# A second set of buffers, a new order of work and smaller on-chip tables in a six-layer local-attention decoder on one Trainium2 core

## The reference

```
x = layernorm(x)
for i in range(6):
    x = attn_layer(shift_tokens(x), Wqkv[i], ...) + x
    x = ffn_layer(shift_tokens(x), ...) + x

attn_layer: q, k, v = split(x @ Wqkv)      # 16 heads of 64
            q, k = l2norm(q) * qs, l2norm(k) * ksc, then rotary tables cos/sin * scale
            out  = softmax(8 q.k within a window of 32 + the 32 before) @ v
            return out @ Wo
ffn_layer:  a, gate = split(layernorm(x) @ W1 + b1)     # 341 each
            return (a * gelu(gate)) @ W2 + b2
result = x_before + that x
```

## Time and profile before

| | |
|---|---|
| median of three runs | 1828.08 us |
| profiled execution, its time | 1832.19 us |
| its span (first to last instruction) | 1830.4 us |
| PE busy | 1636.3 us, 89% |
| DVE busy | 1537.4 us, 84% |
| POOL busy | 1361.2 us, 74% |
| ACT busy | 1188.8 us, 65% |
| stack() begins | at 230.1 us |
| first and last add_attention of a tile | 286.8 and 1784.5 us |

### The profile page before, as it was taken

One profiled execution on the slowest core, in us unless ns is written; L12 is line 12 of the kernel. 1 busy time (PEld: TensorE's weight loads), 2 busy tenths in 40 slices (PEclk: granted clock), 3 DMA queues, 4 the chain that ended last, 5 costly groups with the idle time before them and its releaser, 6 DMA issues.

```text
span 1830.4 us, 77270 instructions
## 1 busy us (share of the span) xinstructions
PE 1636.3 (89%) x32727; PEld 1367.4 (75%) x32727; DVE 1537.4 (84%) x3220; ACT 1188.8 (65%) x2281; POOL 1361.2 (74%) x971
## 2 busy tenths in 40 slices
PE   6688769999989999989999989999899999899985
PEld 4455557788777888878887878888788888788873
DVE  6588779988878999879998979999799899799951
ACT  4465546676666777657767756777676677577651
POOL 4355567788767888778887878888688888788852
PEclk9789979999999999999999999999999999999996
DMA  3644211111221212111213112112112131121101
GB/s 102 253 162 162 81 48 34 41 43 39 92 55 34 54 46 82 53 51 43 54 40 101 40 46 56 47 58 86 43 40 54 40 112 41 45 56 47 37 18 52
DMA packets 81081, 118.47 MB, mean 65 GB/s; under 512 B 41643, under 2 KB 55140, under 8 KB 80612
## 3 DMA queue, kind: packets, MB, share of 16 engines
q1 hardware_dynamic: 80162, 113.27, 21.0%
q10 hardware_dynamic: 578, 0.26, 0.1%
HBM read 38.72 MB, written 21.32 MB: 33 GB/s over the span
## 4 chain that ended last, share of the span: by engine, by line
PE 74%; issue 5%; DVE 4%; DMA 1%; ACT 1%; POOL 1%; SPq 0%; ACTq 0%; DVEq 0%; POOLq 0%
PE banks L1168 10%; PE banks L1181 10%; PE banks L1086 8%; PE banks L1130 7%; PE banks L1088 7%; PE banks L1087 7%; PE banks L1143 5%; PE banks L1098 4%; PE banks L1108 4%; PE banks L1223 4%; PE banks L1198 2%; PE banks L1200 2%; PE banks L1199 2%; DMA wo<-in_L_ffn_Wo_dram 1%; PE banks L1069 1%
## 5 line engine op out<-in xcount | busy, mean ns | idle before, releaser
L1416 POOL TENSOR_TENSOR qk_c<-qk_c,qk_s 128x1024 f32<-128x1024 f32 x192 | 459.2, 2392 | 210.9 <-DVE qk_s L1511 208.1
L1424 POOL TENSOR_TENSOR qk_c<-qk_c,nrm 128x1024 f32<-128x1024 f32 x192 | 362.6, 1905 | 41.0 <-DVE nrm L1559 41.0
L1086 PE MATMUL banks<-high,xT 128*128 128x512 f32 x576 | 270.9, 470 | 19.4 <-DVE qk_s L1511 12.1
L1500 DVE TENSOR_TENSOR qk_c<-banks,rot 128x512 f32<-128x512 f32 x384 | 261.6, 681 | 31.1 <-ACT sq L1289 30.0
L1329 ACT COPY pT<-banks 128x512 f32<-128x512 f32 x192 | 112.7, 587 | 266.2 <-PE banks L1143 266.2
L1511 DVE TENSOR_TENSOR qk_s<-banks,rot 128x512 f32<-128x512 f32 x384 | 261.2, 680 | 0.0
L1289 ACT ACTIVATE sq<-banks 128x512 f32<-128x512 f32 x384 | 237.0, 617 | 23.3 <-PE banks L1088 13.3
L1088 PE MATMUL banks<-high,xT 128*128 128x512 f32 x576 | 231.6, 402 | 0.9 <-issue 0.9
L1518 DVE TENSOR_REDUCE ssq<-sq 128x16 f32<-128x1024 f32 x192 | 232.0, 1208 | 0.0
L1087 PE MATMUL banks<-low,xT 128*128 128x512 f32 x576 | 230.2, 400 | 0.9 <-issue 0.9
L1181 PEld LDWEIGHTS banks<-wo,attT 128*128 128x128 f32 x1536 | 194.9, 200 | 36.5 <-issue 26.3
(11 more groups left out here) (157 smaller groups left out, 3673.7 us busy)
## 6 DMA issues: line engine op xcount, KB each, us to landing
v_back<-v_own SPq DMA_DIRECT2D x96, 384.0 KB, 3.7
front_raw<-in_L_ffn_Wqkv_dram SPq DMA_DIRECT2D x18, 512.0 KB, 5.5
v_back<-v_own SPq DMA_DIRECT2D x72, 128.0 KB, 2.4
w_high<-high SPq DMA_DIRECT2D x15, 512.0 KB, 2.7
w_low<-low SPq DMA_DIRECT2D x15, 512.0 KB, 4.1
high<-w_high SPq DMA_DIRECT2D x15, 512.0 KB, 4.7
low<-w_low SPq DMA_DIRECT2D x15, 512.0 KB, 4.9
wo<-in_L_ffn_Wo_dram SPq DMA_DIRECT2D x6, 512.0 KB, 5.1
```

The lines of the kernel that those rows point to most:

```text
L1086: pe.matmul(bank[n % 2][:, :], xT[:, 1, lo:lo + P], w_hi[:, col:col + 512], start=True, stop=False)
L1416: pool.tensor_tensor(x, x, qk_s[:, kind, :], ALU.add).then_inc(s["rotd"], 1)
L1424: pool.tensor_tensor(x, x, bcast(nrm[:, t % 2, HEADS * kind:HEADS * (kind + 1)], 2, DH), ALU.mult).then_inc(s[("qn", "kn")[kind]], 1)
L1500: dve.tensor_tensor(qk_c[:, t % 2, kind, 512 * half:512 * half + 512].rearrange("p (h d) -> p h d", d=DH), bank[n % 2][:, :].rearrange("p ...
```

## The change

- qT, pT and attT get two buffers (t % 2), sq gets all four halves. The waits for "the last reader is done" move back by one tile. The second half of attend's output goes to bank 5 instead of 3.
- The five bodies get another order. A tile's projections are all of one round now (project(t, 2) to (t, 5) and then (t + 1, 0) and (t + 1, 1)), attend is one round earlier (t - 3), prob_sum and root_step open DVE's round.
- wo gets two buffers; load_wo(layer + 1) is issued at tile 5 of the layer, so a layer ahead.
- rot holds two layers. front() stores the tables of layers 2 to 5 to DRAM, behind the skip, and SP loads one layer's tables at tile 6 of the layer before it.
- The feed-forward's norm weights have a semaphore of their own (ln_in), so that ffn_transpose no longer waits for W1.
- The last two rows' feed-forward jobs use more banks (ffn_bank). The skip is added to the first three rows before the last feed-forward result is there, the last one is added directly, and the result is written in four DMAs.
- SP waits for the scores before it shifts values, and for attend before it shifts a row.

```diff
-            rot=sb("rot", [P, DEPTH, 4, GPB * DH]),
+            rot=sb("rot", [P, 2, 4, GPB * DH]),
+            rot_d=nc.dram_tensor("tables", [DEPTH, P, 4 * GPB * DH], F32, kind="Internal").ap(),
...
+            for layer in range(2, DEPTH):
+                sp.wait_ge(s_const, 2 * layer + 2)
+                sp.dma_start(k["rot_d"][layer, :, :], later[:, layer - 2].rearrange("p k n -> p (k n)")).then_inc(s_tabout, 16)
             sp.wait_ge(s_skip, 16 * BATCH)
+            sp.wait_ge(s_tabout, 16 * (DEPTH - 2))
...
-    wo = sb("wo", [P, PAIRS, D])
+    wo = sb("wo", [P, 2, PAIRS, D])
-    sq = sb("sq", [P, 2, 512])
+    sq = sb("sq", [P, 4, 512])
-    qT = sb("qT", [P, PAIRS, P])
+    qT = sb("qT", [P, 2, PAIRS, P])
-    pT = sb("pT", [P, PAIRS, P])
-    attT = sb("attT", [P, PAIRS, P])
+    pT = sb("pT", [P, 2, PAIRS, P])
+    attT = sb("attT", [P, 2, PAIRS, P])
...
+    def ffn_bank(r, job):
+        if r == NIT - 2:
+            return {"gate0": 0, "gate1": 0, "gate2": 0, "value0": 1, "value1": 1, "value2": 1}.get(job, 7)
+        if r == NIT - 1:
+            return {"gate0": 0, "gate1": 2, "gate2": 4, "value0": 1, "value1": 3, "value2": 7, "out": 5}.get(job, 7)
+        return 7
...
             def shift_values(t):
...
                 sp.wait_ge(s["v_r"], 2 * t + 2)
+                need(sp, s["sc"], min(t, TILES))
...
-                    if layer > 0 and at == 4:
-                        sp.wait_ge(s["wo_p"], BATCH * GPB * layer)
-                        load_wo(layer)
+                    if layer + 1 < DEPTH and at == 5:
+                        need(sp, s["wo_p"], BATCH * GPB * layer)
+                        load_wo(layer + 1)
+                    if 2 <= layer + 1 < DEPTH and at == 6:
+                        sp.wait_ge(s["ab"], 4 * BATCH * GPB * layer)
+                        sp.dma_start(rot[:, (layer + 1) % 2].rearrange("p k n -> p (k n)"), k["rot_d"][layer + 1, :, :]).then_inc(s["rot_in"], 16)
...
             def store_q(t, half):
...
-                need(act, s["sc"], t)
+                need(act, s["sc"], t - 1)
...
             def store_prob(t, half):
...
-                need(act, s["av"], t)
+                need(act, s["av"], t - 1)
...
             def store_att(t, half_w):
...
-                need(act, s["wo_p"], t)
+                need(act, s["wo_p"], t - 1)
...
             def add_ffn(r):
...
+                if r == NIT - 1:
+                    sum_rows()
                 dve.wait_ge(s["w2_p"], r + 1)
-                x = stream[:, (r % BATCH) * GPB:(r % BATCH + 1) * GPB, :]
+                x = stream[:, rows_of, :] if r < NIT - 1 else total[:, rows_of, :]
...
-            dve.tensor_tensor(total, total, stream[:, :, :], ALU.add).then_inc(s["sum_r"], 1)
```

More of the change, by code:

```diff
@@ L997, in load_next @@
             def load_next(layer, n):
[L998 removed]
+                for proj in ("proj0", "proj1"):
+                    sp.wait_ge(s[proj], 3 * (BATCH * GPB * (layer + 1) - 1) + n + 1)
                 load(layer + 1, n)
@@ L1011, in shift_row @@
                 sp.wait_ge(s["added"], GPB * (row + 1))
+                need(sp, s["av"], min(GPB * row + 5, TILES))
                 need(sp, s["f3"], row)
@@ L1180, in out_proj @@
                 for c in range(PAIRS):
-                    last = pe.matmul(bank[7][:, 0:D], attT[:, c, :], wo[:, c, :], start=(c == 0), stop=(c == PAIRS - 1))
+                    last = pe.matmul(bank[7][:, 0:D], attT[:, t % 2, c, :], wo[:, t // (BATCH * GPB) % 2, c, :], start=(c == 0), stop=(c == PAIRS - 1))
                 last.then_inc(s["wo_p"], 1)
@@ L1397, in body @@
-                exponentials(t - 2, 1)
+                squares(t + 1, 1)
+                if j == 2:
+                    store_gate(it - 2, 0)
+                if j == 3:
+                    store_value(it - 2, 1)
+                store_prob(t - 2, 0)
             act.wait_ge(s["zeroed"], 5)
```

261 lines of the change are left out of this document (138 added, 123 removed).

## The result

The changed kernel takes 1807.96 us (median of 12 runs, 1797.27 to 1821.88) against 1830.91 for the kernel before on the same chip (12 runs, 1825.24 to 1833.97). The ratio is 0.9889, with a 95% interval of 0.986 to 0.9918: 1.1% faster, 23 us, where 83 were forecast. The profiled execution of the changed kernel has a span of 1806.3 us.

What follows compares the result with a forecast made beforehand. The prediction took PE, 97% busy, to bound the stack, with DVE close behind. Its terms, -40 - 41 + 6.5 + 3 - 11.5 = -83, gave 1749 us profiled and 1745 as median, range 1716 to 1790.

Steps and rivals of the forecast that it cites:

- The new order, -41: Stack's 23 rows: reordered engine bodies remove DVE's waits, so a row takes 60.1 us, 1.8 less; 41 us saved.
- Rival (a): Stack's rows: the order brings nothing, rows stay at 61.9 us, time 1786; chance 0.18.
- wo a layer ahead, -40: Five layer boundaries: loading wo early removes 8.0 us at each, 40 us saved, with nothing late in its place.
- Values' weights, +3: Layer's end: SP's later shifts delay the values' weight loads, 0.6 us for each of five layers; ends 0 and 15.
- Tables at the front's end, +6.5: Front's end: four uncovered 512 KB table stores delay stack() by 6.5 us, range +4 to +9.
- The tail, -11.5: After the last row: own banks, early skip addition and smaller last DMA save 11.5 us, range 8 to 17.
- the quicker tail: Tail matmuls: fewer gaps lift the clock to 2.4 GHz, some 5 us sooner, at 1740; one chance in five.
- (b): Stack's rows: they reach DVE's floor of 58.4 us, -80 us instead of -41, time 1706; chance 0.13.
- (c): Stack's rounds: a loop through all engines makes them slower; 1860 at 5 us a row; chance 0.04.
- (d): Loads: early wo load queues behind an SP wait, or values' weights come 8 us late per layer; 1785; chance 0.05.
- waits on out_proj and ffn_out near zero: Sign in the stack: DVE's waits for these two PE results, 84.1 and 60.6 us before, nearly vanish.
- distances of 60 us for four tiles: Sign in the stack: add_attention calls four tiles (one row) apart stand 60 us apart.

Runs made afterwards that it cites:

- new_half: Changed kernel with half of the small matmuls of scores and attend replaced by wide ones on zeros (result not the reference's): 1707.89 us, ratio 0.933.
- old_half: old_order with half of the small matmuls of scores and attend replaced by wide ones on zeros: 1730.24 us, ratio 0.9449.
- before_wo2: Kernel before with only two buffers for wo and its load a layer ahead: 1797.66 us, ratio 0.983.
- old_order: Changed kernel with the four engines' order of the kernel before, and attend's second bank 3, put back: 1795.09 us, ratio 0.9817.
- tail_hid16: before_wo2_tail with 16 matmuls of 32 columns at TensorE's very start, where it waits for the first loads: 1837.03 us.
- before_wo2_tail: Kernel before, order untouched, with two wo buffers, wo loaded a layer ahead and the changed kernel's tail: 1787.20 us, ratio 0.9743.
- pad66: Changed kernel with 66 more matmuls of 32 columns on TensorE ahead of the first round: 1828.34 us, ratio 0.9979.
- shift64: Changed kernel with 64 empty instructions on TensorE ahead of the first round: 1805.09 us, ratio 0.9859.
- shift192: Changed kernel with 192 empty instructions on TensorE ahead of the first round: 1805.96 us, ratio 0.9874.
- pad197: Changed kernel with the largest number of extra matmuls of 32 columns on TensorE ahead of the first round, more than pad66: 1893.34 us, ratio 1.0325.

## Why the prediction was right or wrong

**The new order, -41: the step that failed.** The mechanism was right: without stalls the order brings 36.0 us in the rows, and both DVE waits went as the layout said. That 36.0 is near 41 is in part luck. The 16 ordinary rows give 14.2 us, 0.9 each where 1.8 was forecast; the five rows with a layer's start give 17.8 and the last row 4.1. What failed is the sentence "short stalls that no semaphore explains remain as they are". They went from 48.3 us to 88.9, of which by the slope of about 1.1 some 45 us came into the time. The sum of the rows closes within 5 us: 1463.7 - 32.0 (wo, measured alone, with 51.2 us of stalls in it) - 36.0 (order) + 1.1 x (88.9 - 51.2) (stalls) = 1437.2, against 1442.1. The other error stands in "97% busy": PE's busy time was read as a floor of 59.6 us a row. new_half has more to do, and is shown busy for 58.4 in a row of 58.5. And of the 61.9 us that the prediction took for a row of the old order, 48.3 x 1.1 / 23 = 2.3 us were stall (old_half's ordinary rows take 59.4), which no order of waits could bring back. So the 60.1 us were chosen by a floor that isn't one. Rival (a) has it almost word for word ("a stall that moves is still a stall"), and gave 1786 as its time. It was still too low, since the stall grew.

**wo a layer ahead, -40.** Measured alone, -32.0. The wait of five times 5 us is gone, but the rounds at a layer's start kept 1.0 us of their 8.0 in three cases and 2.7 and 3.1 in two. What the 1.0 is stays open, for PE has no wait for a DMA in before_wo2. With the old order and no stalls, values' weights are the next thing late; PE's waits for DMA in old_half (300 to 1700 us):

```profile
PE banks L1111 <- DMA low<-w_low: 9.8, 5, 2.7
```

The prediction said that nothing is late in its place. In old_order, with its stalls, this wait is 3.6 us. In the new order this second cause goes too: the same row of the changed kernel has 0.4 us, and new_half's rows across a layer's start take 0.2 to 0.3 us more than the others.

**Values' weights, +3.** 0.4 us of wait. The layout had DMA landing at 12 and PE needing it at 13, and the margin was enough.

**Tables at the front's end, +6.5.** stack()'s first DMA leaves at 234.49 instead of 230.10: +4.4, inside the range of 4 to 9. This time scatters from run to run: 234.1 to 237.7 where the tables are stored, 229.2 to 231.8 where they are not, and 223.75 in tail_hid16. SP's rows at the place, after and, last, before:

```profile
226.86 0.32 SPq L326 DMA_DIRECT2D skip<-front_pre  x1
227.22 3.00 SPq L330 DMA_DIRECT2D tables<-front_later  x4
234.49 0.38 SPq L987 DMA_DIRECT2D wo<-in_L_ffn_Wo_dram  x1
...
230.10 0.38 SPq L973 DMA_DIRECT2D wo<-in_L_ffn_Wo_dram  x1
```

**Left out: the filling.** The first add comes 11.3 us later, 6.9 more than the tables' 4.4. These 6.9 us belong to the new order, whose first rounds fill a longer pipe. From stack()'s first DMA to the first add it takes 63.7 us (after) and 63.8 (new_half), where the old order takes 56.7 (before), 56.1 (before_wo2_tail), 57.3 (tail_hid16), 56.5 (old_order) and 57.0 (old_half). The prediction had no term for it.

**The tail, -11.5.** -12.9. The gates and values of the last row (timeline of PE; the heads of the first, second, fifth and sixth group of three):

```profile
1790.00 0.77 PE L1222 MATMUL banks<-f_nT_lo,high 128*128 128x512 f32 x1 [2.93 <-issue]
...
1791.41 0.63 PE L1222 MATMUL banks<-f_nT_lo,high 128*128 128x512 f32 x1
...
1794.31 0.39 PE L1222 MATMUL banks<-f_nT_lo,high 128*128 128x512 f32 x1
...
1795.00 0.40 PE L1222 MATMUL banks<-f_nT_lo,high 128*85 128x512 f32 x1
```

The first two stand 1.4 us apart (forecast 1.3), the last two 0.7. The windows show why (clock third from the end):

```profile
1788.00:1793.30 5.30, 3.30 (x8) 2.66 (x9) 0.00 (x0) 1.61 (x3) 1.26 (x1) 0.51 0.01 3
1793.30:1796.00 2.70, 2.56 (x12) 1.53 (x10) 0.00 (x0) 2.48 (x5) 1.30 (x1) 1.00 0.00 0
```

The granted clock was at the 1.2 GHz level while PE came out of its waits, and at 2.4 GHz behind eight matmuls without a gap. This is the quicker tail that the prediction held for one chance in five, by the Trainium skill (TensorE: Matmul & The Clock Gate, the part on the HAM clock gate): the trace agrees with the rule for the second half of the groups. It was worth some 0.4 + 0.6 + 0.6 = 1.6 us in the last three distances (0.93, 0.69, 0.69 against 1.3), and not 5. The small matmuls of pad66 did not lift the clock: it stayed at 0.50 through 26 us of them, though PE is shown as busy throughout.

**The rivals.** (b), rows of 58.4, is what the order does once stalls are gone: 58.5. That DVE is the bound there, as (b) says, is not shown, since PE is as busy. (c), the slower loop, did not show. Nor did (d), wo waits nowhere. Of the forecast's own tests, "waits on out_proj and ffn_out near zero" came true and "distances of 60 us for four tiles" did not; and the sign that was to prove it wrong, DVE waiting for squares, is there with 49.1 us. In new_half, with the same order, it is 13.4 us (300 to 1700):

```profile
DVE qk_c L1537 <- ACT sq L1322: 13.4, 41, 0.9
...
DVE banks L1604 <- PE banks L1157: 1.2, 2, 0.7
```

So most of these waits, too, came with the stalls.

**What stays open.** Why a stall inside the scores costs about 2.2 us and one inside attend about 1.0 (medians over all profiled kernels). Attend's loads run at 1.96 / 128 = 15 ns each and those of the scores at 10, which fits a fetch that partly overlaps, but that was only argued. That the packet is the cause rests on time (all 46 stalls end behind one), on the count of 256 records, on the pace of the 512 records before a border and on new_half; a packet could not be held back or hastened by itself. Why the empty instructions of shift64 take no place in the count is open too.

## What to carry to other kernels

Look for gaps inside a line that one wait has released ("issue" inside a dense group of small matmuls), and sum them before costing a new order: they are a term of their own, and a new order moves them. When two versions differ by less than such a sum (here 48 to 99 us of 1800), compare them with several shifts of TensorE's instruction count, since one alignment tells of luck as much as of the order. And let each part of a large change stand alone once: wo ahead and the new tail gave 45 us together (1832.25 to 1787.20), all parts only 23.

## What the hardware showed

- PE stands still for up to 4.1 us (old_order) with no semaphore to wait for, 1.2 to 1.7 us behind the end of a 16,384-byte packet of the instruction queue q8. All 729 such stalls in the rows of 20 profiled kernels stand at a count of TensorE's records that leaves 193 or 194 when divided by 256 (some 125 weight loads a packet: 262 packets for 32,727).
- In the changed kernel 42 of 54 borders stalled PE where the 512 records before took under 9 us, and 3 of the 186 others. There are none where a tile has 220 weight loads instead of 341.
- 64 to 192 empty instructions on TensorE moved no stall (shift64 to shift192).
- 16 matmuls of 32 columns in idle time at the program's start changed the time by 50 us, 2.8%, more than the whole change.
- 66 fp32 matmuls of 32 columns ahead of the rounds cost 24 to 33 us. The granted clock stayed at the 1.2 GHz level (0.50) through 26 us of them in pad66 and 82 us in pad197, with PE shown as busy for all of that time.
